# Tying bulk weight staging and slot blanking to chunks of a recurrence, in a two-layer mixture-of-experts kernel

## The reference

```python
# layer 0, mixing: RWKV-6, 2 heads of 64, one state per batch and head
kv = ki[:, None] * vi[None, :]
y  = ri @ (S + uh[:, None] * kv)
S  = di[:, None] * S + kv                 # the recurrence over 1024 tokens
x  = x + ga * (group_norm(y) * g @ Wo.T)
# layer 0, experts: 16 experts of width 256, one per token
assign = argmax(h @ router_w);  out = gelu(h @ w1[assign] + b1) @ w2[assign] + b2
x  = x + gb * sigmoid(logit) * out
# layer 1, mixing: second-order linear attention, 16 heads of 32, decay 0.99
# layer 1, experts: 4 live experts of width 704, two per token
h  = silu(x @ w1[e]) * (x @ w3[e]);  y = h @ w2[e];  out = sum over the two of cw * y
```

## Time and profile before

| what | us |
|---|---|
| median of 3 runs | 690.58 |
| lowest and highest of the 3 | 685.58, 691.32 |
| the profiled execution, device time | 684.28 |
| its span, first to last instruction | 682.2 |
| mean granted clock of TensorE | 0.983 of full |

### The profile page before, as it was taken

How to read it: one execution, slowest core, us unless ns; L and a number is a source line. 1 busy time by engine, 2 the same in 40 slices (tenths; PEclk the granted TensorE clock), 3 DMA queues, 4 the chain that set the end, 5 groups by cost and what they waited for, 6 DMA issues and landing times.

```text
span 682.2 us, 26441 instructions
## 1 busy us (share of the span) xinstructions
PE 641.0 (94%) x10978; PEld 547.5 (80%) x10978; DVE 421.7 (62%) x1384; ACT 302.7 (44%) x1017; POOL 254.8 (37%) x387
## 2 busy tenths in 40 slices
PE   5899999999759989999999999999999999999995
PEld 4567777777649977888888888888887999989995
DVE  3777777777633326577777686868676554444442
ACT  1456666643025414545545554545454353333331
POOL 1455666556710031131525252524243432322325
PEclk9899999999969999999999999999999999999999
DMA  7899200000048210000000000000221667566462
GB/s 191 287 299 308 57 3 2 4 6 19 25 137 244 82 43 7 7 9 7 20 12 20 14 18 16 16 16 12 97 77 26 225 223 240 186 214 225 154 241 62
DMA packets 50486, 65.69 MB, mean 96 GB/s; under 512 B 5168, under 2 KB 40208, under 8 KB 47424
## 3 DMA queue, kind: packets, MB, share of 16 engines
q1 hardware_dynamic: 44992, 57.22, 26.8%
q0 software_dynamic: 2912, 6.03, 2.6%
q10 hardware_dynamic: 2464, 0.76, 0.5%
HBM read 49.45 MB, written 18.87 MB: 100 GB/s over the span
## 4 chain that ended last, share of the span: by engine, by line
PE 59%; DVE 2%; DMA 1%; ACT 1%; issue 0%; SPq 0%; DVEq 0%
PE bank L1924 7%; PE quad L1782 6%; PE quad L1906 6%; PE quad L1908 5%; PE bank L1807 4%; PE pair L1744 3%; PE bank L1830 3%; PE quad L1788 2%; PE pair L1746 2%; PE pair L1745 2%; PE bank L1840 2%; PE pair L1769 2%; PE bank L1843 2%; PE bank L1833 2%; PE bank L1926 1%; PE quad L1911 1%
## 5 line engine op out<-in xcount | busy, mean ns | idle before, releaser
L2183 DVE TENSOR_TENSOR h_masked<-quad,const 128x1536 f32<-128x1536 f32 (+2 forms) x66 | 112.6, 1706 | 59.9 <-PE quad L1788 54.1
L2021 ACT ACTIVATE f_sa<-quad 128x256 f32<-128x256 f32 (+1 forms) x115 | 40.3, 352 | 91.6 <-PE quad L1908 75.8
L2202 DVE TENSOR_TENSOR f_hid<-f_sa,quad 128x256 f32<-128x256 f32 (+1 forms) x115 | 43.1, 380 | 53.6 <-ACT f_sa L2021 53.5
L2403 POOL DMA_INDIRECT moe_slots<-g_pay,g_slot x28 | 28.9, 1034 | 77.2 <-PE bank L1852 68.7
L1924 PE MATMUL bank<-wall,f_hid 128*128 128x128 f32 x390 | 50.7, 277 | 1.1 <-DVE f_hid L2205 0.9
L1924 PEld LDWEIGHTS bank<-wall,f_hid 128*128 128x128 f32 x390 | 47.8, 192 | 3.6 <-DVE f_hid L2205 2.8
L1906 PE MATMUL quad<-f_xT,wall 128*128 128x256 f32 (+1 forms) x190 | 50.0, 345 | 0.5 <-DVE f_hid L2202 0.5
L1908 PE MATMUL quad<-f_xT,wall 128*128 128x256 f32 (+1 forms) x190 | 49.2, 341 | 0.0
L1998 ACT ACTIVATE h_gT<-bank 128x128 f32<-128x128 f32 x64 | 17.8, 278 | 66.2 <-PE bank L1833 66.2
L1782 PE MATMUL quad<-h_qk 32*128 32x128 f32 x1024 | 46.5, 296 | 0.3 <-DVE h_masked L2183 0.3
L1782 PEld LDWEIGHTS quad<-h_qk 32*128 32x128 f32 x1024 | 34.3, 185 | 9.5 <-issue 7.0
(11 more groups left out here) (414 smaller groups left out, 1791.2 us busy)
## 6 DMA issues: line engine op xcount, KB each, us to landing
wall<-moe_w SPq DMA_DIRECT2D x23, 1088.0 KB, 5.1
moe_slots<-blank SPq DMA_DIRECT2D x2, 2112.0 KB, 24.4
wall<-in_experts_dram SPq DMA_DIRECT2D x1, 4120.0 KB, 21.8
e_w<-in_experts_dram SPq DMA_DIRECT2D x15, 257.5 KB, 3.3
moe_slots<-blank SPq DMA_DIRECT2D x1, 1984.0 KB, 9.7
moe_slots<-e_yg SPq DMA_DIRECT2D x7, 256.0 KB, 3.7
f_xg<-moe_slots SPq DMA_DIRECT2D x12, 132.0 KB, 4.1
moe_w<-in_moe_w_dram SPq DMA_DIRECT2D x1, 1408.0 KB, 7.2
```

The lines of the kernel that those rows point to most:

```text
L2021: act.activation(sa[g % 3][:, 0:s], up_bank(n, f)[:, 0:s], ACT.Silu).then_inc(f_sa, 1)
L2183: dve.tensor_tensor(masked[k % 4][:, :, a * P:z * P], quad[:, :, a * P:z * P], cst("causal")[:, None, a * P:z * P].to_broadcast([P, HPG, ( ...
L2202: dve.tensor_tensor(hid[n % 2][:, f, 0:s], sa[g % 3][:, 0:s], up_bank(n, f)[:, T1:T1 + s], ALU.mult)\
L2403: pool.indirect_dma_start(out=t["moe1_slots"], out_offset=bass.IndirectOffsetOnAxis(ap=slot[:, b * 2 + k:b * 2 + k + 1], axis=0), in_=pay[ ...
```

## The change

The same transfers with the same sizes are issued by SP, in another order and behind five waits on `s_state`. The blanking of `moe0_slots` comes first. The copies of w3 and w1 wait for the end of chunk 0, those of w2 for chunk 1, the load of `wall` for chunk 2, and the two halves of the blanking of `moe1_slots` for chunks 3 and 4. No instruction of TensorE, VectorE, ScalarE or GpSimd is changed or moved.

```diff
@@ -389,11 +389,15 @@
             sp.dma_start(W1["o"][0:HL_DIM, :, :], turned_wo[P - HL_DIM:P]).then_inc(s_w1, 16)
             sp.wait_ge(s_set, 3)
+            sp.dma_start(t["moe0_slots"][0:USED_ROWS, :].rearrange("(q p) n -> p q n", p=P),
+                         blank[:, 0:1, 0:C].to_broadcast([P, USED_ROWS // P, C])).then_inc(s_slab, 16)
+            sp.wait_ge(s_state, 2)
             staged = t["moe1_w"].rearrange("e p n -> p e n")
             w1, w3 = t["moe_w1"].rearrange("e p n -> p e n"), t["moe_w3"].rearrange("e p n -> p e n")
             sp.dma_start(staged[:, :, 0:F1], w3).then_inc(s_w2, 16)
             sp.dma_start(staged[:, :, F1:F1 + TAIL1], w1[:, :, MAIN1:F1]).then_inc(s_w2, 16)
             sp.dma_start(staged[:, :, F1 + TAIL1:2 * F1], w1[:, :, 0:MAIN1]).then_inc(s_w2, 16)
+            sp.wait_ge(s_state, 4)
             for e in range(E1_LIVE):
                 sp.dma_start(t["moe1_w"][e, :, 2 * F1:2 * F1 + MAIN1].rearrange("p (f n) -> p f n", f=FULL1),
                              t["moe_w2"][e, 0:MAIN1, :].rearrange("(f p) n -> p f n", p=P)).then_inc(s_w2, 16)
@@ -401,11 +405,11 @@
             sp.dma_start(staged[TAIL1:P, :, 2 * F1 + MAIN1:],
                          blank[TAIL1:P, 0:1, 0:C].to_broadcast([P - TAIL1, E1_LIVE, C])).then_inc(s_w2, 16)
-            sp.dma_start(t["moe0_slots"][0:USED_ROWS, :].rearrange("(q p) n -> p q n", p=P),
-                         blank[:, 0:1, 0:C].to_broadcast([P, USED_ROWS // P, C])).then_inc(s_slab, 16)
+            sp.wait_ge(s_state, 6)
             sp.dma_start(wall[:, :, :], t["experts0"].rearrange("e p n -> p e n")).then_inc(s_wall, 16)
             slots = t["moe1_slots"].rearrange("(q k p) n -> k p q n", k=2, p=P)
             for k in range(2):
+                sp.wait_ge(s_state, 8 + 2 * k)
                 sp.dma_start(slots[k], blank[:, k:k + 1, :].to_broadcast([P, SLOTS1 // T1, PAY])).then_inc(s_fill, 16)
```

## The result

The changed kernel takes 695.71 us in the median of 12 runs (692.01 to 703.66), against 688.99 us for 12 runs of the kernel before. The ratio is 1.0098, with a 95% interval of 1.0072 to 1.0123: slower by 1%, which the interval sets clear of no change. One of the 12 (703.66) was a slow execution, and the ratio leaves it out. The profiled execution took 695.34 us with a span of 693.2, against 684.28 and 682.2.

What follows compares the result with a forecast made beforehand. With TensorE busy 641.0 of 682.2 us and bulk traffic ending early, -0.3 and +0.15 summed to -0.15 us: 684.1 for the profiled execution, 689.0 as median, 8 in 10 for 684.0 to 692.5.

Steps and rivals of the forecast that it cites:

- every deadline: Delayed transfers: each lands before its reader or the first send, at least 12 us ahead of the sends; cost 0.
- The stop of line 1063 in chunk 0: TensorE's 0.86 us stop amid equal matmuls: if traffic, 0.64 us go; if first reaching code, gain 0.
- What the later chunks lose: Chunks 3, 4 and 5, newly loaded: each changes by -0.07 to +0.18 us, taken as +0.05, together +0.15.
- What chunk 0 gains: Chunk 0 with rings nearly empty: between -0.64 and 0 us, taken as -0.3.
- Rival B: Chunks 3, 4 and 5: traffic costs 1.92 us each wherever it runs, net +3.8, 693 on the level; chance 0.08.
- Rival C: End of the recurrence, 185 to 200 us: it shifts against TensorE's clock, -1.8 to +2.5 us; chance 0.05.
- The level: Whole kernel: new median put at 689.0 us, between 690.58 (median of three) and 687.9 (mean of four known).

Runs made afterwards that it cites:

- experiment 3: The changed kernel with its five waits moved from the state to the leaf scores' matmuls, in mid chunk: 683.98 us, ratio 0.9928 to the kernel before.
- experiment 6: The kernel before with 32 small matmuls (128 instructions, half a code block) added ahead of chunk 0: 693.25 us, ratio 1.0086 to the kernel before.
- experiment 1: The changed kernel without its five waits on the state, the new order kept: 687.60 us, ratio 0.9986 to the kernel before.
- experiment 2: The changed kernel with only the load of `wall` taken off its wait and put ahead of chunk 0: 691.90 us, ratio 1.0070 to the kernel before.
- experiment 4: The changed kernel with the load of `wall` cut in eight transfers, each issued once the one before has landed: 690.31 us, ratio 1.0029 to the kernel before.
- experiment 5: The changed kernel with 32 small matmuls (128 instructions, half a code block) added ahead of chunk 0: 698.78 us, ratio 1.0186 to the kernel before.

## Why the prediction was wrong

**Right.** SP's issues came at the ends of the chunks, and every deadline held: no engine waited for a blanking, for `wall` or for the staged weights. The stop of line 1063 in chunk 0 was traffic: at idle rings it is gone, both in the changed kernel and in experiment 3. I had left that open.

**The step that failed** is "What the later chunks lose": "a chunk that becomes loaded changes by -0.07 to +0.18". It measured +3.16, +3.46 and +2.75, together +9.4 us in place of +0.15. The bound took DMA share and length of chunks 1 and 2 as all that matters. It did not ask where in the chunk TensorE runs out of code, or how late the next block may come there. In chunk 2 before, the block ends come at 62.5, 69.1 and 77.1 us, over 6 us apart, and a delay of 1.6 us was hidden. In chunk 3 they come at 85.8 and 89.8. Experiment 3 shows that the same chunk at a higher share has no loss if the traffic lies elsewhere in it, and experiment 6 that chunk 1, my proof of "no loss", loses 3.75 us once its block ends move.

**"What chunk 0 gains"** had the right row and the wrong weight. A stop between two equal instructions, with the cause "issue", is hardly a wait for data. I read it as at most 0.64 us that might go, took -0.3, and did not ask what the same stop would do in another chunk. The gain itself is real: in experiment 3, with idle rings in the first half of chunk 0 and the clock whole as before, VectorE's chunk takes 16.23 us (26.89 to 43.12) in place of 16.96. In the profile of the changed kernel it can't be seen, for there the clock is at half for most of chunk 0, which takes 20.1 us (25.7 to 45.8) and not the 16.3 to 17.0 of the forecast. The two pages of the Trainium skill that I weighed there pointed both ways. "DMA: Bandwidth & Descriptors" (queues, rings and completion order), by which code loads share the engines with bulk data, is borne out in kind. Whether its packet-by-packet turn can make one block wait 3.2 us, as the trace has it, no run here shows. "Runtime: NRT & Kernel Launch" (instruction fetch mechanics), by which such loading is mostly hidden, holds with idle rings (no stop in chunks 3 to 5 before) and not beside bulk transfers; there the measurement decides against it.

**Rival B** was the right side and about the right kind: newly loaded chunks pay. I priced it at +1.92 each from chunk 0's idle time and gave it 0.08. It measured 2.75 to 3.46, of which the clock makes a part I did not have. Its reason, a price of traffic wherever it runs, is not what the runs show: in experiment 3 loaded chunks pay nothing. A stop of 0.93 us with no fall of the clock behind it (chunk 1 after) goes with 0.59 us more of chunk; one of 1.80 us with 3.4 us at half clock behind it goes with 3.16.

**Rival C** spoke of the clock at the end of the recurrence. The clock did matter, but in chunks 3 to 5, and between these two profiles also in chunk 0. The mean granted clock fell from 0.983 to 0.969.

**The level** was put at 689.0, and the 12 runs of before gave 688.99; that it met so closely, from four known times 7 us apart, is luck. Part of the spread lies in the front. Chunk 0 ends at 44.37 us in the profile of before, where TensorE's clock was at half for 6.8 us ahead of it (16.8 to 23.7), and at 45.82 and 46.54 in experiments 1 and 2, where it was at half for 17.1 us as in the changed kernel. Experiment 1 runs at the time of before, so the 1.43 us of chunk 0 among the 11.0 us between the two profiles need not be the change's. The medians agree: experiment 1 is 8.1 us under the change (7.7 by the ratios).

## What to carry to other kernels

A load on the DMA engines is not only a question of bandwidth and deadlines: long streams of small matmuls load code over the same engines, so look for stops between equal instructions with no releaser, and count whether they lie a fixed number of instructions apart (here multiples of 256). When bulk transfers are tied to points of the program, tie them to points behind which TensorE works long on few instructions, and not to points ahead of a dense run. A short stop can cost twice its length when the clock falls behind it (1.30 us of stop and 2.7 of chunk in experiment 2). A chunk that stays fast under load proves nothing for its neighbour until their block ends are compared.

## What was not expected of the hardware

- In chunk 3 a 16 KB block of code started to load 0.7 us after TensorE passed a block end with idle rings, and 3.2 us after it while `wall` was moved at 404 GB/s. Idle rings do not always give the short time: at the two ends of chunk 3 in experiment 6 the packet came 2.5 and 3.2 us after the end with idle rings, and TensorE did not stop only because the next ends were 5.0 and 12.1 us away. From the block end to TensorE's going on behind the next one it took 5.8 us in chunk 3 (87.8 to 93.6), 6.7 in chunk 4 and 7.0 in chunk 5.
- Behind stops of 1.3 to 2.4 us the granted clock was at half for 3.4 us in chunks 3 to 5 (experiment 2 has the one of 1.3), and for 10.2 us in chunk 4 of experiment 4 and chunk 3 of experiment 5, at stops of 1.97 and 2.14 us. Behind stops of 0.93 (chunk 1 after) and 0.83 us (chunk 4 of experiment 5) it stayed whole.
- 128 instructions that do next to nothing, put ahead of the recurrence, changed which chunks lose some 3 us or more (4 and 5 before the shift, 1 after it, and 3 in both). Other edits to TensorE's stream may do the same while bulk traffic runs. What stays open is by what rule the code is held back: it started 0.7 us after one block end and 4.3 us after another under the same chained pieces of 0.5 MB (experiment 4). And after the stop in chunk 3 of the changed kernel the next block started only at 100.26 us, 6.6 us after TensorE had gone on, with no DMA packet at all from 96.7 to 100.2.
